# Cross-attention stacks laid out by head: maxima as two half-array matmuls into two banks, scores in half blocks on three banks

## The reference, cut to what matters

```
L=64; S=6272; H=16; DH=8
q = (ln(x) @ Wq + bq)        # 64 x 128, layer 1 also normalises each head of q and k
k = (ctx @ Wk + bk)          # 6272 x 128
v = (ctx @ Wv + bv)
scores  = einsum('bhld,bhsd->bhls', q, k) * DH**-0.5
weights = softmax(scores, axis=-1)
x = x + einsum('bhls,bhsd->bhld', weights, v) @ Wo + bo
```

## Time and profile before

| | |
|---|---|
| median of 3 runs | 354.59 us (348.44 to 356.33) |
| profiled execution, its own time | 352.56 us |
| its span, first to last instruction | 350.8 us |
| PE busy | 309.2 us (88%) |
| PE weight loads | 218.3 us (62%) |
| DVE busy | 220.0 us (63%) |
| ACT busy | 168.7 us (48%) |
| mean granted TensorE clock | 0.911 |

### The profile page before, as it was taken

The page is one execution under the profiler, slowest core; times in us unless marked ns, Lnnn a source line. Parts: engine busy times, 40 slices in busy tenths (PEclk is TensorE's granted clock), DMA queues, the critical chain, the costliest instruction groups (busy, mean ns, idle before and its releaser), DMA issues.

```text
span 350.8 us, 7357 instructions
## 1 busy us (share of the span) xinstructions
PE 309.2 (88%) x3112; PEld 218.3 (62%) x3112; DVE 220.0 (63%) x451; ACT 168.7 (48%) x224; POOL 29.8 (8%) x21
## 2 busy tenths in 40 slices
PE   4999599999999998988775989999999995658976
PEld 2578377777777774445254866777777773135656
DVE  2689756788875112773987897787887203527571
ACT  2555135556556757694953224655646782011000
POOL 1650000000000012332340000000000000000000
PEclk9999758999999999998899898999999998556988
DMA  7745974644300540210045999855599000000000
GB/s 258 260 86 126 260 156 101 131 93 103 87 2 2 183 204 2 46 28 20 0 101 109 202 352 415 206 119 125 129 346 417 7 3 2 0 0 3 0 2 4
DMA packets 8112, 41.09 MB, mean 117 GB/s; under 512 B 2192, under 2 KB 2512, under 8 KB 7568
## 3 DMA queue, kind: packets, MB, share of 16 engines
q1 hardware_dynamic: 7936, 40.32, 40.5%
q10 hardware_dynamic: 144, 0.31, 0.3%
HBM read 21.32 MB, written 0.03 MB: 61 GB/s over the span
## 4 chain that ended last, share of the span: by engine, by line
PE 70%; DVE 17%; ACT 7%; DMA 2%; issue 2%; SPq 1%; POOL 0%; ACTq 0%; DVEq 0%
PE ps L712 68%; DVE arena L471 3%; DVE mx L449 2%; ACT prob L344 2%; DVE arena L468 2%; DMA kst<-arena 1%; DVE mx L443 1%; DMA arena<-in_ctxT 1%; ACT arena L324 1%; SPq L238 1%; PE ps L855 1%; ACT arena L326 1%; SPq L229 1%; PE ps L724 0%; DVE vaug L701 0%
## 5 line engine op out<-in xcount | busy, mean ns | idle before, releaser
L344 ACT ACTIVATE prob<-ps 128x1024 f32<-128x1024 f32 (+1 forms) x104 | 100.6, 976 | 74.5 <-PE ps L712 73.9
L443 DVE TENSOR_REDUCE mx<-ps 128x1 f32<-128x512 f32 (+1 forms) x156 | 95.4, 655 | 30.1 <-PE ps L712 27.1
L712 PE MATMUL ps<-kst,qst 96*128 96x512 f32 (+1 forms) x208 | 74.2, 437 | 7.6 <-DVE qst L431 3.0
L712 PE MATMUL ps<-qst,kst 98*128 98x256 f32 x392 | 74.4, 313 | 2.4 <-DVE qst L438 1.6
L712 PEld LDWEIGHTS ps<-qst,kst 98*128 98x128 f32 x392 | 56.5, 197 | 20.4 <-issue 10.4
L712 PE MATMUL ps<-prob,vaug 128*18 128x128 f32 x1568 | 57.2, 279 | 0.0
L712 PEld LDWEIGHTS ps<-kst,qst 96*128 96x128 f32 x208 | 37.6, 202 | 20.3 <-issue 6.9
L712 PEld LDWEIGHTS ps<-prob,vaug 128*18 128x18 f32 x1568 | 41.1, 99 | 13.0 <-issue 8.5
L449 DVE TENSOR_REDUCE mx<-ps 128x2 f32<-128x1024 f32 (+1 forms) x26 | 29.0, 1158 | 2.3 <-PE ps L712 2.0
L309 ACT ACTIVATE vaug<-ps 128x512 f32<-128x512 f32 (+1 forms) x26 | 14.7, 572 | 23.4 <-PE ps L712 23.3
L462 DVE COPY avsb<-ps 128x256 f32<-128x256 f32 x8 | 3.4, 420 | 31.5 <-PE ps L712 31.5
(11 more groups left out here) (188 smaller groups left out, 266.9 us busy)
## 6 DMA issues: line engine op xcount, KB each, us to landing
kst<-arena SPq DMA_DIRECT2D x48, 192.0 KB, 3.3
kst<-arena SPq DMA_DIRECT2D x48, 128.0 KB, 2.4
arena<-in_experts SPq DMA_DIRECT2D x1, 5760.0 KB, 18.3
kst<-arena SPq DMA_DIRECT2D x24, 144.0 KB, 2.5
w<-in_experts SPq DMA_DIRECT2D x1, 3456.0 KB, 11.2
w<-in_late SPq DMA_DIRECT2D x1, 3284.5 KB, 12.1
arena<-in_experts SPq DMA_DIRECT2D x1, 3072.0 KB, 15.7
arena<-in_ctxT SPq DMA_DIRECT2D x2, 768.0 KB, 8.5
```

What stands on the lines that cost most here:

```text
L344: nc.scalar.activation(prob[:, B % PROBS, 0:w], ps[:, b0:b0 + 2, :].rearrange("p a b -> p (a b)")[:, 0:w], ACT.Exp, scale=XSCALE).then_inc ...
L443: V.reduce_max(mx[:, p, k:k + 1], ps[:, bnk, 0:width(k)], AX).then_inc(max_read, 1)
L712: return mm(out_, lhsT, rhs, start=start, stop=stop, skip_group_check=True)
```

## The change

Rows of the stacks are laid out by channel with four copies each: row 4c holds khi of channel c, 4c+1 klo, 4c+2 khi, 4c+3 ones. A head then fills 32 neighbouring rows and a pair of heads 64. All 128 rows are used by the scores. The ones fill a quarter of the rows and are set once for each of the two `kst` buffers by a memset over the whole buffer, for which the transfers wait (`ones_set`). The shift stands in rows 3 and 7 of each head's queries, added into `qst` by DVE.

- Maxima of a block: two matmuls, one over rows 0 to 63 and one over rows 64 to 127, into two neighbouring banks (4 and 5, or 6 and 7), read by one DVE reduction of 128x1024. A use of two banks waits for the reduction of the use before the last.
- Scores: half blocks of two tiles, one bank each, in turn on banks 0 to 2; ACT's exponential is 128x512. The sums of `weighted` move to bank 3.
- Queries: projected once instead of three times, spread to the rows by a matmul with a 0/1 matrix, then four DVE instructions on 32 rows each. In layer 1 their normalisation works on 64 columns instead of 256.
- Transfers of the stacks of groups 0 and 1 in layer 0 are interleaved, and three loads come behind them.

```diff
-MAX_BANKS = (4, 5, 7)
 PROBS = 3
+SCORE_BANKS = 3
+ACC = 3
+def halves(i):
+    return [(t, min(t + 2, tiles(i))) for t in range(0, tiles(i), 2)]
+def half_no(G, i, h=0):
+    return G * HALVES + 2 * i + h
...
-                for r, src in ((0, khi), (1, khi), (2, klo)):
-                    sp.dma_start(kst[r * GC:(r + 1) * GC, G % 2, a:b].bitcast(F32),
-                                 src[g * GC:(g + 1) * GC, a:b]).then_inc(in_stack[G % 2][k], 16)
+                for c, low in enumerate(KEY_COPIES):
+                    sp.dma_start(kst[c:P:COPIES, G % 2, a:b].bitcast(F32),
+                                 (klo if low else khi)[g * GC:(g + 1) * GC, a:b]).then_inc(in_stack[G % 2][k], 16)
...
+            nc.gpsimd.memset(cols[:, 0:2 * S // 3], 1.0)
+            pool.wait_ge(ln_y, 1)
+            nc.gpsimd.memset(cols[:, 2 * S // 3:S], 1.0).then_inc(ones_set, 1)
...
-                        w = tiles(i) * GQ
-                        b0 = 2 * (B % 2)
-                        nc.scalar.activation(prob[:, B % PROBS, 0:w],
+                        for h, (t0, t1) in enumerate(halves(i)):
+                            n = half_no(G, i, h)
+                            act.wait_ge(scores_done, n + 1)
+                            nc.scalar.activation(prob[:, B % PROBS, t0 * GQ:t1 * GQ],
+                                                 ps[:, n % SCORE_BANKS, 0:(t1 - t0) * GQ],
+                                                 ACT.Exp, scale=XSCALE).then_inc(exp_done, 1)
...
+            def max_pair(n, G, k):
+                stack_there(G, k)
+                if n >= 2:
+                    pe.wait_ge(max_read, n - 1)
                 a, b = k * CW, k * CW + width(k)
-                return one(ps[:, bnk, 0:width(k)], qst[0:QROWS, G % NG, p * P:(p + 1) * P], kst[0:QROWS, G % 2, a:b])
+                for p in range(2):
+                    r = slice(p * P // 2, (p + 1) * P // 2)
+                    last = one(ps[:, 4 + 2 * (n % 2) + p, 0:width(k)], qst[r, G % NG, p * P:(p + 1) * P], kst[r, G % 2, a:b])
+                last.then_inc(max_made, 1)
...
-                if B % (NG * NB) >= 2:
-                    pe.wait_ge(exp_done, B - 1)
+                for h, (t0, t1) in enumerate(halves(i)):
+                    n = half_no(G, i, h)
+                    if n % (NG * HALVES) >= SCORE_BANKS:
+                        pe.wait_ge(exp_done, n - SCORE_BANKS + 1)
...
+                if c == 1 - KEYS_AHEAD:
+                    pe.wait_ge(ev("q0_n"), 1)
+                    pe.wait_ge(ev("spread"), 1)
+                    one(ps[:, 6, GQ:2 * GQ], spread[:, :], q_d).then_inc(ev("q0_rows"), 1)
```

More of the change, by code:

```diff
@@ L68, in slots_of_steps @@
             blocks += len(step)
-            ahead = EARLY_SLOTS + 1 + -(-27 * blocks // NB)
+            ahead = EARLY_SLOTS + 1 + -(-(NB + 1) * blocks // NB)
             upto = min(len(SLOTS) - (blocks < (NG - 1) * NB), ahead)
@@ L98, in tiles @@
     return min(BT, NT - i * BT)
+HALVES = sum(len(halves(i)) for i in range(NB))
 HE_CHUNKS = [(0, 2), (2, 8), (8, 16), (16, 24), (24, E1)]
@@ L250, in _ @@
                     load("early")
[L251 to L257, removed]
+            ahead = 2
+            for k in range(len(KC) + ahead):
+                if k < len(KC):
+                    stack(0, 0, k)
+                if k >= ahead:
+                    stack(0, 1, k - ahead)
+            load("raw1")
+            load("rows")
+            load("small1")
             for g in (2, 3):
@@ L286, in _ @@
             pool.wait_ge(q_ready, 1)
-            for s in range(2):
-                nc.gpsimd.memset(kst[QROWS:KROWS, s, :].bitcast(F32), 1.0).then_inc(ones_set, 1)
-                pool.wait_ge(ones_set, s + 1)
+            nc.gpsimd.memset(kst[:, 1, :].bitcast(F32), 1.0).then_inc(ones_set, 1)
+            pool.wait_ge(ones_set, 2)
             pool.wait_ge(av_done, NG * NB)
@@ L777, in max_pair @@
                 last.then_inc(max_made, 1)
             def scores(G, i):
-                B = NB * G + i
                 if i == 0:
                     pe.wait_ge(shift_ready, G + 1)
-                if B % (NG * NB) >= 2:
-                    pe.wait_ge(exp_done, B - 1)
-                dst = ps[:, 2 * (B % 2):2 * (B % 2) + 2, :].rearrange("p a b -> p (a b)")
-                for t in range(tiles(i)):
-                    a = (BT * i + t) * P
-                    last = one(dst[:, t * GQ:(t + 1) * GQ], kst[0:KROWS, G % 2, a:a + P], qst[0:KROWS, G % NG, :])
@@ L788, in scores @@
-                last.then_inc(scores_done, 1)
+                for h, (t0, t1) in enumerate(halves(i)):
+                    n = half_no(G, i, h)
+                    if n % (NG * HALVES) >= SCORE_BANKS:
+                        pe.wait_ge(exp_done, n - SCORE_BANKS + 1)
+                    for t in range(t0, t1):
+                        a = (BT * i + t) * P
+                        last = one(ps[:, n % SCORE_BANKS, (t - t0) * GQ:(t - t0 + 1) * GQ], kst[:, G % 2, a:a + P],
+                                   qst[:, G % NG, :])
+                    last.then_inc(scores_done, 1)
@@ L864, in _ @@
             pe.wait_ge(in_pack["early"], 16)
-            pe.wait_ge(zeroed, 1)
             for g in range(NG):
-                last = one(ps[0:QROWS, 6, 256 + g * T:256 + (g + 1) * T], view["wq0x3"][:, g * QROWS:(g + 1) * QROWS], yT[:, :])
+                r = slice(g * GC, (g + 1) * GC)
+                one(ps[r, 6, 0:T], view["wq0x3"][:, g * QROWS:g * QROWS + GC], yT[:, :])
+            for g in range(NG):
+                r = slice(g * GC, (g + 1) * GC)
+                last = one(ps[r, 6, T:T + 1], ident[0:QROWS, 0:GC], view["bq0x3"][:, g:g + 1])
             last.then_inc(ev("q0_ps"), 1)
@@ L944, in _ @@
             yT_of("ln3")
-            for g in range(NG):
-                last = one(ps[0:QROWS, 6, g * T:(g + 1) * T], wq1c[:, g * QROWS:(g + 1) * QROWS], yT[:, :])
-            last.then_inc(ev("q1_ps"), 1)
+            one(ps[:, 6, 0:T], wq1c[:, :], yT[:, :]).then_inc(ev("q1_ps"), 1)
             pe.wait_ge(k_rstd, NB)
```

198 lines of the change are left out of this document (107 added, 91 removed).

## The result

The changed kernel took 363.07 us, median of four runs (359.44 to 364.07); the kernel before took 352.01 in four runs beside it. The ratio is 1.035, 95% interval 1.030 to 1.040: slower. It is formed without the slow executions of before, and so stands above the quotient of the two medians; the profiled execution of before is itself one of its slower ones. The profiled execution took 362.9 us with a span of 361.1, against 352.56 and 350.8. Second profiled executions of both kernels, reported at the end of the experiments, have spans of 357.5 and 346.7: 10.8 us apart, where these are 10.3.

The account below looks back on a forecast made before the run. A middle step was taken as a loop through PE and ACT, with ACT's release of PSUM banks on the path. Front 1.3, cross stages 5.8 and layer 1's front 0.3 gave +7.4 on 352.56: 360.0 us, range 347 to 374.

Parts of the forecast that it names:

- Pairs: Two maxima side by side take 0.235 us; with 0.20 at each border, 0.63 between scores instead of 0.47.
- Middle steps: Full steps of a layer's cross stage: 3.38 us instead of 3.21, +0.17 each, about nine a layer, +1.5.
- Opening step: First group's opening step: three pairs of maxima in one burst and reductions of 1.22 behind them, +0.6 us.
- Shifts: Steps around a layer's three shifts give back 0.3 us each, -0.9, as the last reductions get shorter.
- Last group: Steps without maxima wait for a third exponential: 2.83 us instead of 2.50, about five a layer, +1.7.
- Layer sum: Cross-stage terms of one layer, 1.5 + 0.6 - 0.9 + 1.7 = 2.9 us, 5.8 for both layers.
- Layer 0's front: Start to layer 0's first scores: queries ready near 13.9, longer key chunks, stack wait gone; scores near 44.8, +1.3 us.
- Layer 1's front: Before layer 1's scores: borders hidden behind DVE, shorter normalisation and longer stacking cancel, +0.3 us.
- I keep that stretch: The granted clock of 0.50 from 38.90 to 56.00, after idle time, was taken to stay unchanged.
- Rival 3: Clock: low stretch longer or falling again, 3 to 6 us more, 365 (chance 0.10); avoided, 355 (0.07).
- rival 1: Row changes at pairs of maxima are free, no drain and load hidden: -4 us, 348.5; chance 0.20.
- rival 2: Row groups run in series, each pair of maxima costs 0.22 more: about +16 us, 376; chance 0.11.

Follow-up runs that it names:

- the runs on three and four banks: Kernel before with only scores and exponentials changed to half blocks: 361.18 us (ratio 1.031) on three banks, 346.63 us (0.991) on four.
- With fill: Useless 128x256 matmuls added in PE's waits: kernel before 345.37 us (ratio 0.988), changed kernel 357.51 us (no ratio, runs spread too far).
- short chain: Changed kernel with three of the four DVE instructions that place a head's queries left out in layer 1: 361.42 us, ratio 1.032.
- full rows: Changed kernel with each matmul of a pair of maxima over all 128 rows instead of its own 64: 355.82 us, ratio 1.016.
- pairs in series: Changed kernel with both matmuls of a pair of maxima over rows 0 to 63, so not side by side: 403.03 us, ratio 1.148.

## Why the prediction was right, and where it was wrong

The forecast was 360.0 and +7.4; measured were 362.9 and +10.3 in the profiled executions, with a median of 363.07. Sign and mechanism were right: three banks lengthen the last group, a pair costs gaps at its borders, and at equal clock the changed code costs 8.3. The closeness of the sum is partly luck, since inside a layer the terms +1.5 and -0.9 were both wrong and largely cancelled.

- **Pairs.** Side by side for 0.235, with a gap at each border: confirmed. How much of a gap is a drain and how much a weight load no run separates. "At each border" 0.20 was too much: by the trace a pair's way in adds 0.09 and its way out 0.19 between scores; the step arithmetic (last score to pair 0.21, pair to next 0.44) had it right, the words "0.63 instead of 0.47" counted a score's own 0.12 in. In the front, between fp32 chunks, the border cost 0.15 as forecast.
- **Middle steps.** 3.30 for 3.38. Nine steps at +0.09, less what the last two of a group save, come to about nothing a layer, not +1.5.
- **Opening step.** +0.6: at full clock the first three steps take 8.98 against 8.35.
- **Shifts.** "-0.9" was wrong: 15.09 against 15.20 around a shift, 0.1 each.
- **Last group.** +1.7 forecast; 1.58 in layer 0 and 1.83 in layer 1 at full clock. Of the cross stages' 2.3 and 2.7 this is the larger part, and by the runs on three and four banks it is the missing bank. The Trainium skill, "VectorE: DVE Perf Modes", TRN2 errata, would make two halves 1.14, an estimate; here two exponentials of 128x512 took 1.09 and started 0.49 apart, and the last group's step came out at 2.76, below 2.83 and not above it, so the trace's price held.
- **Layer sum.** 2.9 forecast, 2.3 and 2.7 measured at equal clock.
- **Layer 0's front.** Right in all its parts.
- **Layer 1's front.** The step that failed outright: "the shorter normalisation and the longer stacking cancel: +0.3". They do not: +2.45. I never priced the spreading matmul's round trip (0.86) here, though I had in layer 0, nor four DVE instructions of 32x256 at 0.49 in place of 0.28: +1.6 on the chain. Another 0.8 lies between the first maxima and the first scores (18.99 to 19.83). With fill that is 18.09 to 18.35, so some 0.6 of it is PE's clock. Two executions show it alike, and the short chain shows it on the path.
- **Clock.** "I keep that stretch" failed in layer 1. Rival 3's longer stretch came about, in layer 1 instead of layer 0, where it got shorter: in layer 1 PE now waits 1.88 and 3.47 us for the queries (3.15 before), and 10 us more stood at the lower level after the scores began. Filled waits brought those us back, and about as many in the kernel before. But full rows without fill kept the clock there as well, and the mean clocks of their four runs, 0.932 to 0.942, are all above the 0.906 to 0.928 of the changed kernel's. So the waits alone don't settle when it falls; that stays open.
- **Rivals 1 and 2** fall by the gaps of 0.09 and 0.19 and by starts 3 ns apart. Two of their sums were off: rival 1's layer adds up to about -0.6 (nine steps at -0.15, -0.9 at the shifts, +1.7 in the last group), not -1.5, and rival 2's 90 pairs at 0.22 to 20, not 16.

## What to carry to other kernels

Splitting a PSUM area so that it is emptied in smaller pieces paid here only with the number of banks kept: on four banks the halves gained 0.9%, on three they lost 3%. Running two half-array matmuls side by side saves less than it seems when full-array matmuls stand around them, since each change of shape costs a gap (0.09 and 0.19 us here); full rows with zeros in the other half cost the same between scores, and 0.15 less in a key chunk. When a chain behind a layer norm is rewritten, count every round trip to PE and every DVE instruction by its fixed part, whichever layer it stands in, and look at PE's idle time ahead of a PE-bound stage, as useless matmuls there made the kernel before 1.2% faster.

## What the runs showed of the hardware

- The granted clock stood at 0.50 for 54.6 us while PE was marked busy for 50.6 of them (pairs in series). In no other kernel was one such stretch longer than 27.3. What ended it is not known.
- Two executions of one kernel differ by 3.6 us of span (357.5 and 361.1) with the same order of work. Layer 1's cross stage differs by 1.45 (10.2 and 13.7 us at 0.50), the unchanged rest behind it by 2.05 (17.0 and 27.3 us).
- Fewer partitions save DVE nothing: a TENSOR_TENSOR of 256 columns takes 0.40 to 0.42 us on 32, 64 and 96 partitions, a SCALAR_TENSOR_TENSOR of 256 columns 0.48 on 32 and on 64 (with 0.49 from start to start).
- An fp32 matmul of 512 columns costs 0.88 from start to start and shows as two records of 0.59.
